# An audio tower on one core: the memory keys leave PE's key products and get a maximum and an exponential of their own

## The reference, cut to what matters

```python
q, k, v = map(to_heads, (q, k, v))           # (b, H, C, n), n = 375
mk = jnp.broadcast_to(mem_kv[0], (b, H, C, NMEM))
mv = jnp.broadcast_to(mem_kv[1], (b, H, C, NMEM))
k = jnp.concatenate([mk, k], axis=-1)
v = jnp.concatenate([mv, v], axis=-1)
q = jax.nn.softmax(q, axis=-2) * scale
k = jax.nn.softmax(k, axis=-1)               # over 375 + 8 positions
context = jnp.einsum('bhdn,bhen->bhde', k, v)
out = jnp.einsum('bhde,bhdn->bhen', context, q)
```

## Time and profile before

| what | value |
|---|---|
| median of 3 runs | 478.9 us (478.19 to 482.76) |
| profiled execution | 480.63 us |
| its span | 478.8 us |
| PE busy | 421.4 us, 88% of the span |
| PE weight loads | 363.6 us, 76% |
| DVE busy | 361.0 us, 75% |
| ACT busy | 190.6 us, 40% |
| POOL busy | 136.2 us, 28% |
| chain that ended last | PE 59%, DVE 14%, issue 12% |

### The profile page before, as it was taken

How to read it: one execution, slowest core, us unless ns; L and a number is a source line. 1 busy time by engine, 2 the same in 40 slices (tenths; PEclk the granted TensorE clock), 3 DMA queues, 4 the chain that set the end, 5 groups by cost and what they waited for, 6 DMA issues and landing times.

```text
span 478.8 us, 7541 instructions
## 1 busy us (share of the span) xinstructions
PE 421.4 (88%) x2535; PEld 363.6 (76%) x2535; DVE 361.0 (75%) x946; ACT 190.6 (40%) x377; POOL 136.2 (28%) x189
## 2 busy tenths in 40 slices
PE   3976699999999999999999999999996869987790
PEld 2755587898889788978897988789886847776790
DVE  3543867896999799979988998899899456438761
ACT  2412414831582177128604841593154227520000
POOL 4200120013026313530451055007304410004682
PEclk9997899999999999999999999999999979998885
DMA  5674002000100100020002000200000361130133
GB/s 168 155 269 133 1 2 64 2 0 24 43 2 18 43 23 1 18 64 2 2 18 64 2 1 17 65 1 13 6 1 0 80 104 42 41 84 11 31 94 94
DMA packets 30795, 21.57 MB, mean 45 GB/s; under 512 B 4666, under 2 KB 28312, under 8 KB 30390
## 3 DMA queue, kind: packets, MB, share of 16 engines
q1 hardware_dynamic: 27862, 18.73, 13.8%
q0 software_dynamic: 2880, 2.35, 2.1%
q10 hardware_dynamic: 16, 0.02, 0.0%
HBM read 14.41 MB, written 6.62 MB: 44 GB/s over the span
## 4 chain that ended last, share of the span: by engine, by line
PE 59%; DVE 14%; issue 12%; SPq 5%; DMA 4%; POOL 3%; ACT 2%; POOLq 0%; ACTq 0%; DVEq 0%
PE psB L875 7%; PE psB L877 7%; PE psB L876 7%; PE psC L901 6%; PE psC L838 4%; PE psC L1002 4%; PE psC L839 4%; PE psC L840 4%; DMA xt<-in_x 3%; DVE qsum L1403 2%; POOL A L575 2%; PE psC L985 2%; SPq L407 2%; DVE rs L1362 2%; DVE h2b L1293 1%
## 5 line engine op out<-in xcount | busy, mean ns | idle before, releaser
L875 PE MATMUL psB<-W2h,h1l 128*125 128x512 f32 x192 | 79.0, 412 | 0.0
L877 PE MATMUL psB<-W2h,h1h 128*125 128x512 f32 x192 | 77.0, 401 | 0.0
L876 PE MATMUL psB<-W2l,h1h 128*125 128x512 f32 x192 | 76.8, 400 | 0.0
L619 ACT ACTIVATE h2b<-h2b 125x512 f32<-125x512 f32 x48 | 30.3, 631 | 99.7 <-DVE h2b L1286 99.6
L1286 DVE TENSOR_TENSOR h2b<-psB,b2r 125x512 f32<-125x512 f32 x48 | 33.0, 688 | 20.8 <-PE psB L877 20.3
L877 PEld LDWEIGHTS psB<-W2h,h1h 128*125 128x125 f32 x192 | 36.4, 190 | 9.1
L493 POOL TENSOR_TENSOR sg<-euler,sg 125x6 f32<-125x6 f32 x8 | 15.2, 1896 | 98.0 <-DVE sg L1300 98.0
L876 PEld LDWEIGHTS psB<-W2l,h1h 128*125 128x125 f32 x192 | 36.7, 191 | 7.9
L875 PEld LDWEIGHTS psB<-W2h,h1l 128*125 128x125 f32 x192 | 36.6, 191 | 8.0 <-DVE h1l L1277 0.2
L614 ACT ACTIVATE h<-psA,b1c 128x376 f32<-128x376 f32 x64 | 36.0, 580 | 15.2 <-PE psA L840 14.9
L1293 DVE CUSTOM_DVE_ANT_0 h2b<-h2b,W3r 125x512 f32<-125x512 f32 x48 | 32.3, 684 | 2.8 <-ACT h2b L619 2.7
(11 more groups left out here) (248 smaller groups left out, 1004.2 us busy)
## 6 DMA issues: line engine op xcount, KB each, us to landing
xt<-in_x SPq DMA_DIRECT2D x8, 375.0 KB
xs<-in_x SPq DMA_DIRECT2D x8, 312.5 KB
slot_x<-ebr SPq DMA_DIRECT2D x2, 960.0 KB, 9.2
basef<-in_L_tok_W SPq DMA_DIRECT2D x1, 1024.0 KB, 6.1
ebr<-in_L_ffn_expert_b SPq DMA_DIRECT2D x1, 1024.0 KB, 6.8
ewf<-slot_x SPq DMA_DIRECT2D x2, 480.0 KB, 6.3
h2b<-slot_x SPq DMA_DIRECT2D x2, 480.0 KB, 8.1
slot_y<-h SPq DMA_DIRECT2D x4, 240.0 KB, 2.5
```

What stands on the lines that cost most here:

```text
L619: nc.scalar.activation(slot, slot, ACT.Gelu).then_inc(c_g2.sem, 1)
L875: mm(ps, lo, W2h[:, k, :], start=k == 0, stop=False)
L876: mm(ps, hi, W2l[:, k, :], start=False, stop=False)
L877: last = mm(ps, hi, W2h[:, k, :], start=False, stop=k == HK - 1)
```

## The change

PE no longer copies the memory keys into the key banks. The negated maximum over the memory keys, `nmm`, is taken once in the setup. For each pair DVE takes the maximum over the 375 row columns into `nkt` and combines it with `nmm` by a minimum into `nkm`, one column wide. Behind the fourth pair, `memory_max` adds `nkm` to the 32 memory columns of all pairs (`em`). ACT takes the exponential of each pair over 375 columns, and, behind `route_exp`, one exponential over the 32 memory columns (`memory_exp`). `key_sum` adds up the memory part, adds it to the accumulated one, and then takes the reciprocal. The last transposed block of keys waits for the memory's exponential too.

```diff
@@ key_exp, memory_exp (ACT)
-                after(act, c_km, b, p + 1)
+                after(act, c_kmm, b, p + 1)
                 if prev is not None and p == 0:
                     after(act, c_kt, prev, KJ)
-                    after(act, c_rk, prev, 1)
-                nc.scalar.activation(ek[:, p, :], bank_k(b, p)[:, 0:NK], ACT.Exp, bias=nkm[:, p:p + 1],
-                                     accum_out=ksum[:, p:p + 1]).then_inc(c_ke.sem, 1)
+                    after(act, c_ks, prev, 2)
+                nc.scalar.activation(ek[:, p, 0:G], bank_k(b, p)[:, 0:G], ACT.Exp, bias=nkm[:, p:p + 1],
+                                     accum_out=kst[:, 0, p:p + 1]).then_inc(c_ke.sem, 1)
+
+            def memory_exp(b):
+                after(act, c_em, b, 1)
+                nc.scalar.activation(ek[:, :, G:NK], em[:], ACT.Exp).then_inc(c_kme.sem, 1)
...
@@ step (ACT)
                 if k is not None:
                     route_exp(k, before(k))
+                if f is not None:
+                    memory_exp(f)
                 if m is not None:
                     gelu2(m, 4)
...
@@ keys, k_transposed (PE)
-                split(bank[:, 0:G + 1], Wqh[:, w], Wql[:, w], xh[:], xl[:])
-
-                mm(bank[:, G:NK], ident[:], mkv[:, 0, p, :], start=True, stop=True).then_inc(c_k.sem, 1)
+                split(bank[:, 0:G + 1], Wqh[:, w], Wql[:, w], xh[:], xl[:]).then_inc(c_k.sem, 1)

             def k_transposed(b, prev, j):
                 after(pe, c_ke, b, 4)
+                if j == KJ - 1:
+                    after(pe, c_kme, b, 1)
...
@@ setup (DVE)
                 dve.wait_ge(s_const, N_CONST)
+                vec.tensor_reduce(nmm[:], mkv[:, 0], AX.X, ALU.max, negate=True).then_inc(s_prep, 1)
...
@@ key_max, memory_max (DVE)
                 after(dve, c_k, b, p + 1)
-                if prev is not None:
-                    after(dve, c_ke, prev, 4)
-                vec.tensor_reduce(nkm[:, p:p + 1], bank_k(b, p)[:, 0:NK], AX.X, ALU.max, negate=True).then_inc(c_km.sem, 1)
+                vec.tensor_reduce(nkt[:, p:p + 1], bank_k(b, p)[:, 0:G], AX.X, ALU.max, negate=True).then_inc(c_km.sem, 1)
+                after(dve, c_km, b, p + 1)
+                if prev is not None:
+                    after(dve, c_ke, prev, PAIRS)
+                vec.tensor_tensor(nkm[:, p:p + 1], nkt[:, p:p + 1], nmm[:, p:p + 1], ALU.min).then_inc(c_kmm.sem, 1)
+
+            def memory_max(b, prev):
+                after(dve, c_kmm, b, PAIRS)
+                if prev is not None:
+                    after(dve, c_kme, prev, 1)
+                vec.tensor_tensor(em[:], mkv[:, 0], nkm[:].unsqueeze(2).to_broadcast([128, PAIRS, NM]), ALU.add).then_inc(c_em.sem, 1)
...
@@ key_sum (DVE)
-                after(dve, c_ke, b, 4)
+                after(dve, c_kme, b, 1)
+                vec.tensor_reduce(kst[:, 1, :], ek[:, :, G:NK], AX.X, ALU.add).then_inc(c_ks.sem, 1)
+                after(dve, c_ke, b, PAIRS)
+                after(dve, c_ks, b, 1)
+                vec.tensor_tensor(ksum[:], kst[:, 0, :], kst[:, 1, :], ALU.add).then_inc(c_ks.sem, 1)
+                after(dve, c_ks, b, 2)
                 if prev is not None:
                     after(dve, c_ms, prev, 1)
                 vec.reciprocal(rk[:], ksum[:]).then_inc(c_rk.sem, 1)
...
@@ step and ending (DVE)
                     for p in range(1, PAIRS):
                         key_max(f, before(f), p)
+                    memory_max(f, before(f))
                 if k is not None:
                     route(k, before(k))
```

More of the change, by code:

```diff
@@ L165, in audio_tower @@
         rq = sb("rq", [TP, GJ * HEADS])
+        nkt = sb("nkt", [128, PAIRS])
         nkm = sb("nkm", [128, PAIRS])
+        nmm = sb("nmm", [128, PAIRS])
+        em = sb("em", [128, PAIRS, NM])
+        kst = sb("kst", [128, 2, PAIRS])
         ek = sb("ek", [128, PAIRS, NK])
@@ L255, in audio_tower @@
         c_q = counted("c_q", 3); c_qm = counted("c_qm", 3); c_qs = counted("c_qs", 3)
-        c_k = counted("c_k", 4); c_km = counted("c_km", 4); c_ke = counted("c_ke", 4)
+        c_k = counted("c_k", 4); c_km = counted("c_km", 4); c_kmm = counted("c_kmm", 4); c_em = counted("c_em", 1); c_ke = counted("c_ke", 4); c_kme = counted("c_kme", 1); c_ks = counted("c_ks", 2)
         c_qe = counted("c_qe", 3); c_qsum = counted("c_qsum", 1); c_rq = counted("c_rq", 1); c_qn = counted("c_qn", 1)
@@ L1699, in ending @@
                     key_max(f, k, p)
+                memory_max(f, k)
                 normal2(k, r)
@@ L1763 @@
 N_WR = 12
-N_PREP = 8
+N_PREP = 9
 _INS = ['x', 'L0_tok_W1', 'L0_tok_b1', 'L0_tok_W2', 'L0_tok_b2', 'L0_tok_W3', 'L0_tok_b3', 'L0_attn_norm_w',
```

## The result

The changed kernel takes 485.9 us (median of 6 runs, 482.67 to 487.97); the kernel before, run beside it, 479.0 (6 runs, 478.19 to 482.76). The ratio is 1.0126 [1.0088, 1.0164]: slower by a little over 1%. The time lies inside my range, 2.7 us above the number. The mechanism of the steady rows came as forecast; several sizes did not, and the ending came out the other way.

A forecast was written before the change was run, and what follows sets the result against it. PE and DVE taking turns bound the kernel: five steady rows +4.15 us, the first 0, the last +0.55, row 7's keys -0.4, total +4.3, taking the median from 478.9 to 483.2 us; range 480.2 to 487.0.

The forecast's parts named there:

- What bounds the kernel: Steady rows: PE and DVE take turns; added DVE time counts per row, PE's saving only as far as DVE is ready.
- The keys' stage: DVE before `route`: combines and memory addition add 0.81 us; slack swallows half, so the last bias starts 0.40 us late.
- the rival in which it holds the next maximum: Keys' stage: the next maximum waits for the combine's end; 1.36 us a steady row, 486.4 us in all; chance 0.12.
- the rule on draining: Mechanism of that rival on DVE: a next operation doesn't start before the pipe is empty, semaphore or not.
- The slack of 0.41 us: DVE before layer 2's last bias: it could start at 225.86 but starts at 226.27.
- PE's wait: Before the position product: PE, ready 0.7 us early, waits for `route`'s one-hot through POOL's counts; the saved 0.68 becomes wait.
- The key sum: DVE ahead of the query sum: one reciprocal becomes reduction, addition, reciprocal, each waiting for the last; +0.43 us, no slack.
- The steady sum: Five steady rows at 0.40 + 0.43 = +0.83 us each: +4.15 us.
- The last step: Last row, with no x to split and DVE's slack 0.69 us: 0.81 - 0.69 + 0.43 = +0.55 us.
- The ending: Row 7's keys among the expert products, where PE is the limit: fewer products save time, -0.4 us.
- the rival of the clock: PE's waits per row grow, the granted clock falls: 1.3 us a fall, one to five falls, 484.5 to 490; chance 0.12.
- ScalarE: Table load, `gelu2` and four GELUs start some 0.64 us later; layer 1 still ends before the query transposes, cover 0.42 us.

The follow-up runs named there:

- the one execution against it: The kernel before with one needless 125x512 addition on DVE ahead of the last row's query sum, delaying its last scan: 480.2 us (1 run).

## Why the prediction was right or wrong

**What bounds the kernel: right.** The turns between PE and DVE carried the whole steady part. PE's saving was worth nothing while DVE was late, shown by putting it back, and 0.61 us a row when DVE was not, shown by taking it alone.

**The keys' stage: right.** Forecast +0.81 us before `route`, measured 2.95 - 2.14 = 0.81. The combine came as forecast (0.16 us long, next maximum 0.65 behind the last), so the rival in which it holds the next maximum is refuted by the timeline, and so is the rule on draining as I had put it, without its exception: the operations at 128.04 and 128.16 start before their predecessors end, at 128.13 and 128.24. (The Trainium skill, "VectorE: DVE Perf Modes", "The DRAIN you can't avoid", allows for operations that are not held; taken by itself its rule would have them wait.) The slack of 0.41 us swallowed what it should, and in the steady rows that leaves +0.40. By the Trainium skill's table (same page, "The TRN2 errata"), an estimate of 61 ns, the combine would have been 0.1 us shorter; the trace has 0.16, and so bears out the section's own remark that measured durations are longer than that row.

**PE's wait: right in kind, smaller than the 0.7 us or more I named.** It is 0.49 to 0.52 us in the undisturbed rows, 0.66 in one with a pause.

**The key sum: too small.** Forecast +0.43, measured +0.49: from the reduction to the addition it is 0.28 us from start to start, where I had taken 0.23 from the earlier trace rows. By the landmarks an undisturbed steady row is +0.88 instead of +0.83, 0.25 us in five rows.

**The steady sum: +5.20 instead of +4.15.** 4.40 are five undisturbed rows; about 0.8 are the three pauses (0.29 + 0.17 + 0.35), a term that I did not have. The kernel before has a pause in this part as well, of 0.19 us, which its slack hides.

**The last step: +0.96 instead of +0.55.** This step of the forecast failed: it took the bias to be what the rest waits for, and it is the position product. `route` ends later, the one-hot is counted on POOL, and `pp` waits. PE's and DVE's timeline of the changed kernel:

```profile
364.55 0.21 DVE L1544 TENSOR_TENSOR oh<-rank,rm 125x48 bf16<-125x48 f32 x1
364.68 1.28 DVE L1298 TENSOR_TENSOR h2b<-psB,b2r 125x512 f32<-125x512 f32 x2
364.84 0.80 POOL L529 TENSOR_TENSOR cnt<-cnt,oh 125x16 bf16<-125x16 bf16 x3 [9.83 <-DVE oh L1544]
365.75 0.21 PE L1044 MATMUL psC<-oh,tri_b 125*125 125x48 bf16 x1 [1.29 <-DVE oh L1544]
366.05 0.21 DVE L1548 TENSOR_TENSOR pp<-psC,oh 125x48 f32<-125x48 f32 x1
366.53 0.17 DVE L1558 TENSOR_SCALAR keep<-pos 125x3 f32<-125x3 f32 x1
366.79 0.19 DVE L1441 TENSOR_REDUCE kst<-ek 128x4 f32<-128x32 f32 x1
```

The second bias ends at 365.96 and could be overlapped by 0.07, as in the steady row; `pp` starts 0.16 us later than that. Another 0.18 lies between `keep` and the key sum (0.26 us from start to start, 0.08 in the steady row); it is a fourth pause, with an instruction packet 0.70 us behind it (367.49), and it comes again in the repeated run. In the kernel with its code shifted this step takes 47.19 us instead of 47.41. With 0.06 for the key sum that makes 0.40 of the 0.41.

**The ending: +1.37 instead of -0.4, the wrong way.** The step that failed is the rival of the clock. It was priced well, at 1.3 us a fall, and got a chance of 0.12 because no new wait would be over about 1 us. But an existing wait of PE, 3.33 us long, grew to 3.99 with DVE's lateness, and the stretch at 1.2 GHz around its end was 6.8 us instead of 3.4: +1.18 us up to the query transposes, which is all of the +1.14. I had weighed the waits that each row would gain and did not ask how the long one would grow. That the longer wait made the longer stretch is likely by the table and not shown, by the one execution against it. Behind the first expert transpose the forecast saving was there in part, -0.25 us up to row 6's choice (zero with PE's product kept). From that choice to the end the changed kernel takes 0.5 us more than the one before (50.3 and 49.9), but this last part took 49.0 to 50.5 us in the other kernels (the one with only the product gone left aside), so what is left of the saving at the end can't be told.

**ScalarE: right.** The table load starts 4.43 us behind the first key maximum (131.82 less 127.39), 3.86 before (224.99 less 221.13): 0.57 later, forecast 0.64, and the steady row shows no wait for it. With only the product gone the row became 0.61 us shorter and ScalarE didn't hold it either, where I had expected it to from 0.4 on.

**The number** was low by 2.7 us in the medians: 3.2 in my sum, of which 1.1 goes with the clock, 0.8 is the three pauses of the steady rows, 0.6 the ending's saving, 0.4 the last step (half of it the fourth pause), 0.3 the key sum. That the time fell inside the range is partly luck: the four pauses, 1.0 us, were in none of its cases, and the clock's 1.1 only in a rival that I gave 0.12.

## What to carry to other kernels

Where two engines take turns, first ask at each crossing which one is late and by how much: work taken from the other is worth nothing, and an operation of 0.16 us costs 0.20 us where the next needs it, 0.08 to 0.11 where it does not. So before an exchange of a product for several short operations, count these by their pitch, not their length, and put each behind what another engine waits for: the same addition cost 0.23 us ahead of `route` and 0.11 behind it. Where slack is used up, small pauses that it hid begin to count: look for them in the profile of before, too. And a forecast to within 1% needs the spread of the granted clock at each long wait of PE, of those that are already there above all; one profile doesn't show it.

## What the runs showed of the hardware that I had not expected

- DVE had pauses of 0.17 to 0.35 us at fixed instructions. They were the same in a repeated run within 0.03 us and moved when 32 instructions were put ahead of them. Each was followed within 0.6 to 1.3 us by an 8 KB packet of the instruction queue 14, and these packets came at the same counts of DVE's instructions, some 128 apart, in the changed kernel and in the shifted one.
- Around the end of the same wait of PE, with the same work behind it, the clock was at 1.2 GHz for 3.4 or for 6.8 us, and the way to the query transposes took 5.6 to 5.9 us or 6.7 to 7.2.
- Short DVE operations (0.16 to 0.20 us) start 0.08 to 0.11 us apart where they don't need each other, before their predecessors have ended, and 0.20 to 0.28 us apart where they do.
